# Unread closing matmuls behind the last value step of an attention and expert layer

## The reference

```python
def _L0_attn_ref(x, Wq, Wk, Wv):
    q = (x @ Wq.T).reshape(B, S, H, Hd)
    k = (x @ Wk.T).reshape(B, S, H, Hd)
    v = (x @ Wv.T).reshape(B, S, H, Hd)
    energy = jnp.einsum('bqhd,bkhd->bhqk', q, k)
    attn = jax.nn.softmax(energy / jnp.sqrt(jnp.float32(D)), axis=-1)
    return jnp.einsum('bhqk,bkhd->bqhd', attn, v).reshape(B, S, D)
...
h = jax.nn.silu((x @ w1 + b1) * (x @ w3 + b3))   # each expert
y = h @ w2 + b2
...
xn = _layernorm(x, axis=-1)
x = x + attention(xn) + (weighted sum of two routed experts + shared expert)(xn)
```

## Time and profile before

| what | before |
|---|---|
| median of three runs | 2126.17 us |
| lowest and highest run | 2124.88 and 2126.78 us |
| span of the profiled execution | 2124.5 us |
| TensorE busy (matmul) | 2105.7 us, 99% of the span |
| ScalarE busy | 2015.3 us, 95% |
| VectorE busy | 806.5 us, 38% |
| share of TensorE in the chain that ended last | 93% |

### The profile page before, as it was taken

How to read it: one execution, slowest core, us unless ns; L and a number is a source line. 1 busy time by engine, 2 the same in 40 slices (tenths; PEclk the granted TensorE clock), 3 DMA queues, 4 the chain that set the end, 5 groups by cost and what they waited for, 6 DMA issues and landing times.

```text
span 2124.5 us, 38290 instructions
## 1 busy us (share of the span) xinstructions
PE 2105.7 (99%) x15722; PEld 967.1 (46%) x15722; DVE 806.5 (38%) x1561; ACT 2015.3 (95%) x2228; POOL 251.7 (12%) x260
## 2 busy tenths in 40 slices
PE   9999999999999999999999999999999999999998
PEld 6734444444444444444444444444444444444442
DVE  8554233333333333333333333333333322244531
ACT  6799999999999999999999999999999999999998
POOL 0307673000000000000000000000000000122230
PEclk9999999999999999999999999999999999999999
DMA  8774433122222213222222231313122221322321
GB/s 294 276 260 123 132 108 115 39 75 51 79 59 70 65 47 79 66 65 71 56 63 64 66 72 53 86 44 79 51 79 60 71 68 57 90 78 85 105 91 42
DMA packets 223350, 187.80 MB, mean 88 GB/s; under 512 B 110471, under 2 KB 192190, under 8 KB 223174
## 3 DMA queue, kind: packets, MB, share of 16 engines
q1 hardware_dynamic: 209350, 148.68, 25.2%
q0 software_dynamic: 12496, 36.34, 5.3%
q10 hardware_dynamic: 1328, 0.33, 0.1%
HBM read 130.21 MB, written 55.05 MB: 87 GB/s over the span
## 4 chain that ended last, share of the span: by engine, by line
PE 93%; ACT 3%; DVE 2%; DMA 1%; issue 0%; SPq 0%; DVEq 0%; ACTq 0%
PE PS L887 44%; PE PS L874 31%; PE PS L899 12%; PE PS L911 6%; ACT probs L1171 2%; DMA qk_parts<-part_a 1%; DVE stats L1297 0%; DVE probs L1321 0%; DVE x_parts L1333 0%; DMA resid<-in_x 0%; PE PS L778 0%; DVE part_a L1340 0%; PE PS L780 0%; PE PS L779 0%; DVE mv L1300 0%
## 5 line engine op out<-in xcount | busy, mean ns | idle before, releaser
L1171 ACT ACTIVATE probs<-PS 128x1024 f32<-128x1024 f32 x2048 | 1921.3, 1038 | 72.5 <-PE PS L874 43.6
L887 PE MATMUL PS<-probs,v_head 128*32 128x512 f32 x8192 | 988.5, 599 | 1.0 <-ACT probs L1171 0.8
L874 PE MATMUL PS<-q_ring,k_stack 50*128 50x512 f32 x4096 | 729.2, 442 | 6.2 <-ACT probs L1171 4.4
L874 PEld LDWEIGHTS PS<-q_ring,k_stack 50*128 50x128 f32 x4096 | 332.1, 184 | 607.2 <-ACT probs L1171 544.1
L887 PEld LDWEIGHTS PS<-probs,v_head 128*32 128x32 f32 x8192 | 211.3, 108 | 447.8 <-issue 372.8
L1634 DVE TENSOR_SCALAR gate_in<-PS,bias_sb 128x256 f32<-128x256 f32 (+7 forms) x165 | 76.4, 463 | 604.1 <-PE PS L899 595.7
L899 PE MATMUL PS<-x_hi,w_hi 128*128 128x256 f32 (+9 forms) x660 | 199.3, 302 | 0.0
L1243 POOL DMA_DIRECT2D slot_y<-y_sb x39 | 27.9, 716 | 1409.3 <-DVE y_sb L1704 1373.0
L899 PE MATMUL PS<-x_hi,w_lo 128*128 128x256 f32 (+9 forms) x660 | 185.0, 280 | 0.0
L899 PE MATMUL PS<-x_lo,w_hi 128*128 128x256 f32 (+9 forms) x660 | 184.2, 279 | 0.0
L899 PEld LDWEIGHTS PS<-x_hi,w_hi 128*128 128x128 f32 (+1 forms) x660 | 118.7, 180 | 53.1 <-issue 53.1
(11 more groups left out here) (199 smaller groups left out, 1143.8 us busy)
## 6 DMA issues: line engine op xcount, KB each, us to landing
w_raw<-in_w SPq DMA_DIRECT2D x110, 352.0 KB
k_stack<-qk_parts SPq DMA_DIRECT2D x120, 128.0 KB
w_raw<-in_w SPq DMA_DIRECT2D x55, 256.0 KB
q_ring<-qk_parts SPq DMA_DIRECT2D x372, 32.0 KB
qk_parts<-part_a SPq DMA_DIRECT2D x20, 512.0 KB, 4.9
slot_x<-early_sq SPq DMA_DIRECT2D x39, 256.0 KB, 3.9
slot_in<-slot_x SPq DMA_DIRECT2D x156, 64.0 KB, 2.6
slot_y<-y_sb POOLq DMA_DIRECT2D x39, 256.0 KB, 2.5
```

The lines of the kernel that those rows point to most:

```text
L874: last = pe.matmul(bank(2 * score_buffer(turn, g) + r), k_stack[rows, kt * P:(kt + 1) * P], q_ring[rows, sweep, i * QC:(i + 1) * QC], star ...
L887: last = pe.matmul(bank(O_BANK)[VW * j:VW * (j + 1), :], v_head[:, kt, :], probs[:, slot, (j % 2) * QC:(j % 2 + 1) * QC], start=(kt == 0), ...
L1171: nc.scalar.activation(probs[:, prob_slot(g), :], bank(2 * score_buffer(h, g), 2), ACT.Exp, scale=ENERGY_SCALE).then_inc(s_exp, 1)
```

## The change

Behind the last loop, the changed program of TensorE waits for all exponentials (`s_exp`), for all expert results to be taken (`s_yc`) and for VectorE's transposition of the last output (`s_osb`). Then it issues 102 matmuls whose results nothing reads. They reuse operands that lie in SBUF, and write banks 0 to 5, bank 6 and bank 7. A new semaphore, `s_probe`, is raised by TensorE and waited for by TensorE; three of these waits make it wait until its own work so far is complete.

```diff
+        s_probe = sem("s_probe")
...
             while issued[1] < SWEEPS * NT:
                 next_scores(2)
                 next_values(1)
+
+            pe.wait_ge(s_exp, H * GH)
+            pe.wait_ge(s_yc, UNITS)
+            pe.wait_ge(s_osb, SWEEPS)
...
+            def half_scores(r, b, kt):
+                rows = slice(r * HALF, r * HALF + ROWS)
+                return pe.matmul(bank(b), k_stack[rows, kt * P:(kt + 1) * P], q_ring[rows, 1, 0:QC], start=True, stop=True)
+
+            def half_up(r, n):
+                return pe.matmul(f_half(0), w13_hi[0][side(r), 0, n % DT, 0:P], x_hi[side(r), (n % DT) * CH:(n % DT + 1) * CH],
+                                 start=(n == 0), stop=(n == 11))
+
+            def pairs(n):
+                for k in range(n):
+                    half_scores(0, 2 * (k % 3), k)
+                    last = half_scores(1, 2 * (k % 3) + 1, k)
+                return last
+
+            def steps(n, halves):
+                for k in range(n):
+                    parts = halves if k else 1
+                    cols = QC // parts
+                    for i in range(parts):
+                        for j in range(QCH):
+                            last = pe.matmul(bank(O_BANK)[VW * j:VW * (j + 1), i * cols:(i + 1) * cols], v_head[:, k, :],
+                                             probs[:, j // 2, (j % 2) * QC + i * cols:(j % 2) * QC + (i + 1) * cols],
+                                             start=(k == 0), stop=(k == n - 1 and i == parts - 1))
+                return last
+
+            pairs(6)
+            steps(2, 1)
+            pairs(3).then_inc(s_probe, 1)
+            pe.wait_ge(s_probe, 1)
+            for n in range(6):
+                half_up(0, 2 * n)
+                half_scores(1, n % 5, n)
+                half_up(0, 2 * n + 1)
+            half_scores(0, 5, 0).then_inc(s_probe, 1)
+            pe.wait_ge(s_probe, 2)
+            for n in range(6):
+                half_scores(0, n % 5, n)
+                half_up(1, 2 * n)
+                half_up(1, 2 * n + 1)
+            pe.wait_ge(s_probe, 2)
+            half_scores(0, 5, 0)
+            steps(3, 2).then_inc(s_probe, 1)
+            pe.wait_ge(s_probe, 3)
+            for n in range(12):
+                pe.matmul(f_half(1), w13_hi[0][:, 0, n % DT, 0:P], x_hi[:, (n % DT) * CH:(n % DT + 1) * CH], start=(n == 0), stop=(n == 11))
+            pairs(3)
```

More of the change, by code:

```diff
@@ L1033, in _, with side @@
                 next_values(1)
+            pe.wait_ge(s_exp, H * GH)
+            pe.wait_ge(s_yc, UNITS)
+            pe.wait_ge(s_osb, SWEEPS)
+            def side(r):
+                return slice(r * HALF, (r + 1) * HALF)
+            def half_scores(r, b, kt):
[40 more added lines that the diff above has]
+            pairs(3)
         @block.scalar
```

## The result

The changed kernel took 2136.78 us (median of three runs, 2135.16 to 2137.15) against 2126.17 us: a ratio of 1.0045 with a 95% interval from 1.0031 to 1.0059, so 10.6 us more, where 9.9 were forecast (2136.1 us, range 2134.4 to 2139.8). The profiled execution took 2136.78 us with a span of 2134.8 us, 10.3 above the span of before.

The account below looks back on a forecast made before the run. TensorE is busy 99% of the span but idle for its last 5.1 us, of which some 3.8 us hide added work. The added chain moves the end by 9.9 us: 2126.17 + 9.9 = 2136.1 us, range 2134.4 to 2139.8.

Parts of the forecast that it names:

- the output's landing: Kernel's end: added work from 2120.32 to 2124.10 would be free, some 3.8 us; everything beyond pushes the end out.
- Steps 2 to 9: Added TensorE chain from the six score pairs to the end of the last three pairs, 2120.33 to 2134.07.
- step 1: After VectorE's transposition: TensorE resumes 0.11 us later, at 2120.33.
- the first mixed stretch: Six groups of one score matmul beside two half experts, then one score matmul: 1.88 us, plus 0.11 for the wait.
- the second: Second mixed stretch, with row halves mirrored, and one score matmul, up to the value step: 1.81 us.
- the three value steps: Behind the mixed stretches, second and third step in column halves: 2.78 us, halves costing nothing more.
- the whole-array matmuls: Twelve whole-array expert matmuls, up to the score pairs behind them: 1.59 us.
- The waits of TensorE for itself: In the added work: 0.11 us for each of the three waits that bite, between zero and 0.2.
- The closing: From TensorE's last matmul to the end of the span: 0.3 us, between 0 and 0.4.
- Rival A: Mixed stretches: the halves run one after the other, 2.9 us more, 2139.0 us; chance 0.16.
- Rival B: Mixed stretches: weight loads of the 24 half experts show, 1.9 to 4.1 us more, 2138.0 to 2140.2; chance 0.06.
- Rival E: Added work: the clock falls to 0.50 from about 2122.8, remaining 11.3 us up to twice as long, about 2147; chance 0.03.

Follow-up runs that it names:

- covered: Changed kernel with only six score pairs and one full value step left of the added work; 2127.33 us, ratio 0.9998 to the kernel before.
- edge: Changed kernel with only six score pairs, two value steps and three pairs left of the added work; 2122.19 us, ratio 0.9996 to the kernel before.
- again: The changed kernel rerun unchanged; 2136.77 us, ratio 1.0042 to the kernel before.
- again2: The changed kernel rerun unchanged once more, in another group; 2133.44 us, ratio 1.0050 to the kernel before.
- quarters: Changed kernel with the last two of the three value steps in column quarters instead of halves; one profile, 2.81 us for the three steps.
- same_half: Changed kernel with each mixed group's score matmul moved into the row half of its half experts; 2142.80 us, ratio 1.0073 to the kernel before.
- both_long: Changed kernel with twelve groups instead of six in both mixed stretches, still across the row halves; 2134.40 us, ratio 1.0050 to the kernel before.
- late_wait: Changed kernel with the added work waiting for VectorE's last addition instead of the transposition; 2136.80 us, ratio 1.0058 to the kernel before.

## Why the prediction was right

**The mechanism.** Nothing ahead of the last value step was changed by the edit; what was added went behind it, and all of it beyond the output's landing was paid in full. SyncE's last wait for TensorE's queue shows it, against 0.2 us before: 0.5 in `covered`, 2.2 in `edge` and 11.6 in the change, each with a fall in the block, and 10.0 in `again`, `again2` and `quarters`, without one. The forecast of 9.9 makes 10.1 of it at full clock.

**The terms.** Steps 2 to 9 summed to 13.74 us and took 13.74 in `again2` and 13.7 in `again`, so here the number was met for the stated reasons. One by one in the profile of the change: resuming 0.11 (step 1, forecast 0.11); the first mixed stretch with its wait 2127.29 - 2125.31 = 1.98 (1.99); the second 2129.11 - 2127.29 = 1.82 (1.81); the three value steps 2.79 (2.78); the whole-array matmuls 2133.61 - 2131.99 = 1.62 (1.59); the last pairs 0.98 (0.96). The waits of TensorE for itself took 2125.31 - 2125.24 = 0.07 and 2131.99 - 2131.90 = 0.09, a little less than 0.11. The closing took 2134.8 - 2134.59 = 0.2 (0.3).

**The weakest term held.** That a score matmul and two half experts share the array side by side was inferred from like pairs. `same_half` is its counter-test: 0.48 for a group in one half, 0.23 across. Rival A fails by that. The 0.48 is also no more than 0.23 + 2 x 0.12 for the matmuls alone, so no load shows even where all three stand in one half. Rival B, the rule in the Trainium skill ("TensorE: Matmul & The Clock Gate", Part 3: Packing small matmuls) that a weight load overlaps only matmuls of other row groups, fails with it: in the change, groups with three weight loads followed each other every 0.23 us, with two of the loads behind matmuls of the same half (the row of PEld at 2125.90 above).

**What was mis-sized.** Rival E. I gave a fall of the clock 3 in 100 and 11.3 us, as if it had to last to the end. It happened in 3 of the 8 profiles whose block resumes after the pause of 0.92 us (the change, `covered` and `edge`; not `again`, `again2`, `quarters`, `both_long`, nor at the start of `same_half`), and then lasted 3.4 us and cost 1.6. The step that failed is the sentence that a pause of 1.7 us left the clock alone. It was misread: in the earlier trace rows 1.73 us is how long the weight loads had been idle, while the matmuls had been idle for 0.85. So the rows shown had no pause of the matmuls as long as the new one of 0.92 with the clock at 1.00 behind it. In the three profiles the fall began 0.1 to 0.6 us after the block resumed. Which of the pauses brings it (0.83 us ahead of the last value step, 0.92 behind it, or both) stays open.

**What was luck.** The forecast for the profiled execution hit partly because two deviations met: in the profile of the change the fall added 1.6 us, while the last value step started 1.1 us earlier than before (2117.28 against 2118.38) and the closing was 0.1 shorter. 9.9 + 1.6 - 1.1 - 0.1 is the 10.3 that the spans differ by. The prediction left open what the 0.4 to 2.3 us between the profiled span and the three runs are. Each run of the change is 2.0 us longer than its own span (2136.78 and 2134.8, 2135.16 and 2133.2, 2137.15 and 2135.2), so what differs from 2.0 is scatter between executions. Since 9.9 was added to the median, the sum didn't suffer.

## What to carry to other kernels

Price work behind the last result against the landing of the output, in time order: it is free up to there, and then costs all of its length. Take the price of work that runs side by side from start-to-start distances, not from means. In this kernel, cutting value steps into column halves or quarters cost at most 0.03 us for three steps, and short matmuls in one row half were free beside a long one in the other. Read idle time on the row of the matmuls and not on that of the weight loads. Where TensorE gets new pauses, give a spell at half clock a chance of its own (here 3 of 8 profiles, 1.6 us each) and don't assume that it lasts to the end.

## What the runs showed of the hardware that was not expected

- TensorE's clock fell from 2.4 to 1.2 GHz although TensorE was busy 4.80 of 4.90 us by the profile, when its matmuls used one row half at a time (profile of `same_half`; the mean clocks of its four runs fit); across both halves it stayed at 2.4 GHz for 6.5 us (profile of `both_long`).
- It also fell in the middle of the kernel, near 1755 and 1762 us, in the stretch with expert matmuls of 32 columns, which take 0.11 us each, almost as long as those of 256. TensorE was busy all the time ahead of these falls. Of the eleven profiles with these narrow matmuls, five have a fall there. With 256 columns in their place no run out of 11 had a mean clock below 0.999. Why it falls there in some runs and not in others of the same program stays open. A third place was seen once, at 95.0 us in the front part (`late_wait`), after a stretch in which TensorE was busy 1.95 of 3.40 us.
- Each such spell lasted 3.4 or 6.8 us and cost close to half of that where TensorE was busy: 1.6 us for each fall of 3.4 us in the block. One or two of them in some runs and none in others make an estimated 1.6 to 3.2 us of scatter, 0.08% to 0.15%: more than the difference that some of these experiments asked about, so for those the profile decides and not the time.
